# Thirty-three full expert tiles of five batches, not twenty-five of four, inside the last routing round, and a cadence of four tiles for the last stages

## The chip, the core and the metric

The kernel runs on one core of a Trainium2 chip. The metric is the device time of one execution in microseconds (us). TensorE (PE) multiplies, VectorE (DVE) and ScalarE (ACT) read its results out of PSUM, GpSimd (POOL) issues the indirect DMAs, and SyncE (SP) issues the plain ones.

## What is computed

Eight batches of 512 tokens of width 128 go through an attention block and then a mixture-of-experts block. Only the second half of that matters here: each token picks two of eight experts, and its two results are added, weighted by the gate, to a kept row.

```python
probs = softmax(t @ router_w)                      # 8 experts
vals, idx = top_k(probs, 2)
w = vals / sum(vals)                               # gate
hid = silu(t @ w1[e]) * (t @ w3[e])
y = sum over the two experts of w * (hid @ w2[e])
out = x + layernorm(res + y)                       # the last stage of a batch
```

## The kernel before

**Rounds.** A batch passes four stages, a, p, m and f, one round each, and each round runs the stages of up to four batches side by side. Stage f routes a batch: it finishes the attention output, normalises, takes the two best experts of each token (on DVE), ranks the tokens within their expert, and sends 8 blocks of 128 token rows to `token_rows` in HBM (`f_send0` to `f_send7`, on POOL). The last round holds stage f of batch 7 alone.

**Tiles.** All routed rows are worked in 71 tiles of 128 rows of one expert. A tile step k does, on PE, the transpose of tile k's rows (L1109), the eight matmuls of the hidden layer of tile k-1 (`hidden`, L1116) and those of the output of tile k-3 (`down`, L1125). I call the start of the transpose of step k T(k). ACT copies the transposed rows, copies the expert's weights (L1263) and does the silu (L1248). DVE begins its step k with `take_dest` of tile k (L1753, L1754; it waits for the tile's rows and for the send of tile k-8, whose buffers it takes over), then does `gated` of tile k-1 (L1759) and `result` of tile k-3 (L1764, into `k_rows`). POOL sends the result of tile k-3 to `result_rows` with one indirect DMA (L1360). `hidden` of tile n needs `gated` of tile n-2. SP loads the rows of tile k when tile k-8 has been transposed (`load_rows`, L772), so it runs eight steps ahead.

**Early and late tiles.** The rows of the first `SOON` = 4 batches fill at least 4 x 8 - 7 = 25 whole tiles (`EARLY`). Those can start before batch 7 is routed. The other 46 need the counts of all batches: DVE plans them (`plan3` to `plan8`), and SP waits for the plan and for all sends before it loads the first of them. `LAST_ORDER` is a table that writes out for each engine where its tile steps stand between the steps of stage f in the last round. `GROUPS` says at which tile steps PE, ACT and SP read the next tile numbers into registers.

**Last stages of a batch.** When a batch's results are in HBM, SP loads them in two halves (`load_results`, L787, 2 DMAs of 128 KB each, after the wait for the sends of the first `tiles_before_end_of(b)` tiles). DVE adds the two results (`add_pair`, L1771), adds the kept row (`add_kept`, L1775), takes statistics (L1781) and mean and variance (L1788 to L1792), POOL raises to the power -1/2 (`invert`, L1369), ACT centres the four blocks (L1269), and DVE scales and adds (`finish`, L1799). `FINAL_AT[b]` is the step number of batch b, and each part has a lag to it. A step number n there is the tile step k = n + 2. So DVE adds the pair in step FINAL_AT + 2, SP loads in its step FINAL_AT + 5 (POOL's `invert` too), and DVE finishes in step FINAL_AT + 11.

```python
FINAL_AT = [41 + 5 * b for b in range(NB - 1)]
LOAD_AT, SUM_AT, STATS_AT, MEAN_AT, POW_AT, CENTRE_AT, OUT_AT, STORE_AT = 3, 1, 2, 3, 3, 4, 9, 20
def tiles_before_end_of(b):
    return EARLY + NE if b < SOON - 1 else NE * (b + 1) + NE - 1
```

## Time and profile before

| | |
|---|---|
| three runs | 698.15, 699.35 and 699.73 us, median 699.35 |
| the profiled execution | 696.38 us, its span 694.2 us |
| PE, busy share of the span | 88% |
| DVE | 73% |
| ACT | 59% |
| POOL | 49% |
| mean granted TensorE clock | 0.934 |

The profiled execution is 2.97 us below the median of the three runs, and 2.2 us of it lie outside the span. The tiles begin at 544.2 us of the span. The busy shares are averages over stages that have different limits; in the stretch of the tiles the waits and the order of each engine's queue tell more than the shares.

### The profile page before, as it was taken

The numbers are of one execution on the slowest core, as the hardware profiler recorded it, in microseconds if no ns is written. First come the engines' busy times: TensorE is split into PE (matmuls) and PEld (weight loads), VectorE is DVE, ScalarE is ACT, GpSimd is POOL, SyncE is SP. The second block draws the span as 40 slices with busy tenths as digits, with TensorE's granted clock in tenths as the row PEclk, the third lists the DMA queues.
The fourth block names the chain that finished last, engine by engine and source line by source line (L and its number), as shares of the span: only waits on it lengthen the run. The fifth ranks groups of instructions, "written<-read, shape, count | busy, mean of one in ns | idle before, by whom it ended". The sixth has DMA issues, their size and how long they took to land.

```text
span 694.2 us, 15645 instructions
## 1 busy us (share of the span) xinstructions
PE 609.9 (88%) x5186; PEld 364.6 (53%) x5186; DVE 506.8 (73%) x1616; ACT 412.0 (59%) x826; POOL 339.6 (49%) x388
## 2 busy tenths in 40 slices
PE   8887599999999899999999999879998887899980
PEld 3444345455545455454544545434343486899970
DVE  4456877786897898689779878677688356457894
ACT  3223158566658656565765657454564676688971
POOL 0043246058527835752873565165014056767783
PEclk9988879999999999999999999977898999999995
DMA  6200000000100000010000001001232013345653
GB/s 174 78 0 1 0 1 1 2 1 1 35 2 1 14 23 1 1 35 3 1 19 19 1 1 35 2 2 36 77 109 70 14 58 111 99 113 166 176 156 91
DMA packets 35616, 30.05 MB, mean 43 GB/s; under 512 B 6160, under 2 KB 32720, under 8 KB 35520
## 3 DMA queue, kind: packets, MB, share of 16 engines
q1 hardware_dynamic: 31216, 19.65, 10.1%
q0 software_dynamic: 4320, 9.38, 4.0%
q8 instruction: 45, 0.74, 0.4%
q14 instruction: 35, 0.29, 0.1%
HBM read 17.54 MB, written 12.57 MB: 43 GB/s over the span
## 4 chain that ended last, share of the span: by engine, by line
PE 64%; DVE 14%; ACT 9%; issue 7%; POOL 5%; DVEq 0%; POOLq 0%; ACTq 0%
PE wide L1116 9%; PE small L933 7%; PE small L921 5%; PE wide L895 4%; PE wide L1125 4%; ACT pT L1216 4%; PE wide L868 4%; PE wide L886 4%; PE wide L843 3%; PE small L957 3%; PE wide L877 3%; PE small L986 3%; PE small L971 2%; DVE nmax L1421 2%; PE small L1010 2%
## 5 line engine op out<-in xcount | busy, mean ns | idle before, releaser
L1421 DVE TENSOR_REDUCE nmax<-wide 128x2 f32<-128x256 f32 (+3 forms) x256 | 200.1, 817 | 43.7 <-PE wide L886 42.5
L1216 ACT ACTIVATE pT<-wide 128x1024 f32<-128x1024 f32 (+1 forms) x192 | 161.6, 883 | 41.3 <-PE wide L895 40.4
L1360 POOL DMA_INDIRECT result_rows<-k_rows,dest x71 | 69.9, 984 | 49.5 <-DVE k_rows L1764 26.6
L933 PE MATMUL small<-pT,v_pad 128*5 128x512 f32 (+3 forms) x1024 | 85.2, 478 | 2.7 <-ACT pT L1216 2.7
L1351 POOL DMA_INDIRECT token_rows<-m_row,place_u x64 | 62.5, 977 | 45.4 <-issue 16.4
L1302 POOL TENSOR_TENSOR a_rstd<-a_ve,neg_half 128x4 f32<-128x4 f32 x16 | 16.5, 1029 | 117.3 <-DVE a_ve L1407 117.3
L895 PE MATMUL wide<-qT,kT 32*128 32x384 bf16 (+3 forms) x512 | 71.5, 312 | 0.0
L886 PE MATMUL wide<-kT,qT 32*128 32x256 bf16 (+3 forms) x512 | 70.5, 314 | 0.0
L877 PE MATMUL wide<-future_T,idb 128*128 128x128 bf16 (+1 forms) x384 | 62.6, 246 | 7.9 <-DVE nmax L1421 4.6
L868 PE MATMUL wide<-future_sb,idb 128*128 128x128 bf16 (+1 forms) x384 | 64.1, 250 | 5.7 <-ACT pT L1216 2.8
L1145 ACT ACTIVATE oT_g<-small 128x512 f32<-128x512 f32 x32 | 19.1, 597 | 79.7 <-PE small L933 79.7
L933 PEld LDWEIGHTS small<-pT,v_pad 128*5 128x5 f32 x1024 | 25.8, 92 | 59.8 <-issue 50.3
L1759 DVE TENSOR_TENSOR a_work<-a_work,wide 128x256 f32<-128x256 f32 x71 | 29.7, 418 | 32.6 <-PE wide L1125 16.7
L877 PEld LDWEIGHTS wide<-future_T,idb 128*128 128x128 bf16 x384 | 28.6, 99 | 36.4 <-issue 15.8
L1125 PE MATMUL wide<-a_p_sb,a_work 128*128 x284 | 43.2, 275 | 0.6 <-DVE k_rows L1764 0.6
L1116 PE MATMUL wide<-a_work,p_hT_sb 128*128 128x128 f32 x280 | 38.0, 279 | 4.8 <-ACT a_work L1242 3.5
L868 PEld LDWEIGHTS wide<-future_sb,idb 128*128 128x128 bf16 x384 | 29.8, 101 | 22.7 <-issue 11.5
L1116 PE MATMUL wide<-a_work 128*128 128x128 f32 x288 | 38.8, 278 | 2.4 <-issue 2.2
L1125 PEld LDWEIGHTS wide<-a_p_sb,a_work 128*128 128x128 f32 x284 | 37.3, 192 | 0.8 <-issue 0.8
L1116 PEld LDWEIGHTS wide<-a_work,p_hT_sb 128*128 128x128 f32 x280 | 34.0, 192 | 7.0 <-ACT a_work L1242 4.4
L1116 PEld LDWEIGHTS wide<-a_work 128*128 128x128 f32 x288 | 35.3, 193 | 3.4 <-issue 3.0
L895 PEld LDWEIGHTS wide<-qT,kT 32*128 32x128 bf16 x512 | 20.1, 92 | 29.6 <-issue 16.8
(254 smaller groups left out, 1260.6 us busy)
## 6 DMA issues: line engine op xcount, KB each, us to landing
a_qkv_sb<-token_rows SPq DMA_DIRECT2D x71, 72.0 KB, 1.8
x<-L_attn_x SPq DMA_DIRECT2D x8, 256.0 KB, 3.4
w<-L_ffn_w SPq DMA_DIRECT2D x2, 1024.0 KB, 7.3
out<-x SPq DMA_DIRECT2D x16, 128.0 KB
result_rows<-k_rows,dest POOLq DMA_INDIRECT x71, 2.6
token_rows<-m_row,place_u POOLq DMA_INDIRECT x64
a_p_sb<-L_ffn_w SPq DMA_DIRECT2D x8, 128.0 KB, 4.6
yin_own<-result_rows SPq DMA_DIRECT2D x8, 128.0 KB
```

What stands on the lines that cost most here:

```text
L868: pe.matmul(bank[:, i * T + lo:i * T + lo + len(blocks) * P], idb[:, :], future_sb[:, 0:len(blocks), :], start=True, stop=False, skip_grou ...
L877: pe.matmul(diagonal, idb[:, :], future_T[:, :, :] if len(blocks) > 1 else future_T[:, 0, :], start=True, stop=False, skip_group_check=True)
L886: return pe.matmul(bank_of(ring, max_name(g, n))[:, at:at + keys], qT1[rows, m.parity, g, tile * P:(tile + 1) * P], kT[rows, m.parity, g, ...
L895: return pe.matmul(bank_of(ring, exp_name(g, s))[:, at:at + queries_from(tile)], kT[rows, m.parity, g, tile * P:(tile + 1) * P], qT2[rows, ...
L921: last = pe.transpose(bank[0:rows, t * P:(t + 1) * P], source(t), ident)
L933: last = pe.matmul(bank[32 * r:32 * r + HD + 1, k * P:T], v_pad[:, m.parity, k, g * R + r, :], probs, start=(k == 0), stop=(k == NT - 1), ...
L1116: last = pe.matmul(wide[:, tile.half, j * P:(j + 1) * P], w_now[tile.half][:, j * P:(j + 1) * P], x_T[:, tile.half, :], start=True, stop=True)
L1125: last = pe.matmul(y_bank(tile), hid_T[:, tile.half, h * P:(h + 1) * P], w2_sb[:, e, h, :], start=(h == 0), stop=(h == FH - 1))
L1216: act.activation(pT[:, g % 2, part, at:at + n].rearrange("p (n q) -> p n q", n=2), in_, ACT.Exp, scale=SCALE_B).then_inc(ring.free(step), 1)
L1351: pool.indirect_dma_start(token_rows[:, :], bass.IndirectOffsetOnAxis(ap=place_u[:, n, t:t + 1], axis=0), m_row[:, n, t, :], None).then_in ...
L1360: pool.indirect_dma_start(result_rows[:, :], bass.IndirectOffsetOnAxis(ap=dest[:, tile.buf:tile.buf + 1], axis=0), y_rows[:, tile.buf, :], ...
L1421: ins = dve.tensor_reduce(nmax[:, tile, heads], bank[:, :, at:at + keys_up_to(tile)], AX, ALU.max, negate=True)
```

## The change

`SOON` goes from 4 to 5. So `EARLY` goes from 25 to 33 and `LATE` from 46 to 38. The last round holds 33 tile steps instead of 25, and `LAST_ORDER` is written anew. The reads of tile numbers stand at steps 0, 24, 33 and 57 (before: 0, 25 and 49). The padding rows are written at SP's step 29 (before: 21). The last stages of batches 0 to 6 start at step numbers 45, 49, 53, 57, 61, 65, 69 (before: 41, 46, 51, 56, 61, 66, 71). Since `EARLY` grows, the load of batches 0 to 3 waits for the first 41 tiles (before: of batches 0 to 2 for the first 33).

```diff
 LAST_ORDER = {
     "PE": """
-        tile f_pv2 tile f_o1 f_pv3 tile f_o2 f_o3 tile f_oT tile f_up tile tile tile f_tT tile f_logits
...
+tile f_pv2 tile f_o1 f_pv3 tile tile f_o2 f_o3 tile f_oT tile f_up tile tile tile tile f_tT tile tile f_logits tile tile f_rank tile tile tile tile tile tile tile plan tile tile tile tile tile tile tile tile tile tile tile""",
...
-SOON = 4
+SOON = 5
 EARLY = SOON * NE - (NE - 1)
 LATE = TILES - EARLY
...
-PADS_AT = 21
-GROUPS = {0: EARLY, EARLY: 24, EARLY + 24: LATE - 24}
+PADS_AT = 29
+GROUPS = {0: 24, 24: EARLY - 24, EARLY: 24, EARLY + 24: LATE - 24}
...
-FINAL_AT = [41 + 5 * b for b in range(NB - 1)]
+FINAL_AT = [45 + 4 * b for b in range(NB - 1)]
...
-    b = (n - lag - FINAL_AT[0]) // 5
+    b = (n - lag - FINAL_AT[0]) // 4
...
-                experts.update(read_tiles(pe, 1, 0, EARLY, NE - 1))
+                experts.update(read_tiles(pe, 1, 0, GROUPS[0], NE - 1))
```

The POOL queue in the last round, from the tile results behind stage f's `m_row` on (three more stand ahead of that before, five now). `token_rows` are the sends of batch 7, `result_rows` those of tiles, and `a_rstd` and `p_rstd` are what `invert` writes. Before:

```order
L1360 DMA result_rows<-k_rows,dest 10112x128 x4
L1351 DMA token_rows<-m_row,place_u 34688x144 x3
L1360 DMA result_rows<-k_rows,dest 10112x128
L1351 DMA token_rows<-m_row,place_u 34688x144 x2
L1360 DMA result_rows<-k_rows,dest 10112x128
L1351 DMA token_rows<-m_row,place_u 34688x144 x2
L1360 DMA result_rows<-k_rows,dest 10112x128
L1351 DMA token_rows<-m_row,place_u 34688x144
L1360 DMA result_rows<-k_rows,dest 10112x128 x34
L1369 TENSOR_TENSOR a_rstd<-a_ve,neg_half 128x4
L1360 DMA result_rows<-k_rows,dest 10112x128 x5
L1369 TENSOR_TENSOR p_rstd<-p_ve,neg_half 128x4
```

The same place of the POOL queue in the changed kernel:

```order
L1355 DMA result_rows<-k_rows,dest 10112x128 x5
L1346 DMA token_rows<-m_row,place_u 34688x144 x3
L1355 DMA result_rows<-k_rows,dest 10112x128
L1346 DMA token_rows<-m_row,place_u 34688x144 x2
L1355 DMA result_rows<-k_rows,dest 10112x128 x2
L1346 DMA token_rows<-m_row,place_u 34688x144 x2
L1355 DMA result_rows<-k_rows,dest 10112x128
L1346 DMA token_rows<-m_row,place_u 34688x144
L1355 DMA result_rows<-k_rows,dest 10112x128 x34
L1364 TENSOR_TENSOR a_rstd<-a_ve,neg_half 128x4
L1355 DMA result_rows<-k_rows,dest 10112x128 x4
L1364 TENSOR_TENSOR p_rstd<-p_ve,neg_half 128x4
```

Ten tile results stand ahead of the first token send now, not seven; one more tile result stands between the sends; and from the first `invert` on there are four tile results from one to the next, not five.

DVE's queue in the steps of batch 0's `finish`, where the names are those of the batches' result buffers (`yin_own` of batches 0 and 1, `kT` of 2 and 3). Before, with `finish` in a step of its own:

```order
L1759 TENSOR_TENSOR a_work<-a_work,wide 128x256
L1764 TENSOR_SCALAR k_rows<-wide,a_qkv_sb 128x128
L1753 COPY a_qkv_sb<-a_qkv_sb 128x1
L1754 CAST dest<-a_qkv_sb 128x1
L1799 SCALAR_TENSOR_TENSOR x<-yin_own,a_rstd,x 128x128 x4
L1759 TENSOR_TENSOR a_work<-a_work,wide 128x256
```

And in the changed kernel:

```order
L1754 TENSOR_TENSOR a_work<-a_work,wide 128x256
L1759 TENSOR_SCALAR k_rows<-wide,a_qkv_sb 128x128
L1748 COPY a_qkv_sb<-a_qkv_sb 128x1
L1749 CAST dest<-a_qkv_sb 128x1
L1770 TENSOR_TENSOR kT<-kT,res 128x512
L1794 SCALAR_TENSOR_TENSOR x1<-yin_own,a_rstd,x1 128x128 x4
L1754 TENSOR_TENSOR a_work<-a_work,wide 128x256
```

`finish` now falls into the same step as the `add_kept` of the batch two later, and no step is left without a part of a last stage.

## Rows read from the trace of the kernel before

**Rows 1.** Timeline of PE, last round: start, length, line, operation, [idle before <-releaser].

```profile
565.03 0.66 PE L921 MATMUL small<-idf,m_row 128*128 128x128 f32 x4 [1.12 <-POOL m_row L1343]
...
571.95 0.19 PE L1068 MATMUL small<-sel,before_sb 128*128 128x32 bf16 x1 [1.06 <-DVE sel L1604]
...
595.95 1.13 PE L1116 MATMUL wide<-a_work,p_hT_sb 128*128 128x128 f32 x8 [0.94 <-ACT a_work L1242]
...
601.14 0.30 PE L1109 MATMUL wide<-idf,a_qkv_sb 128*128 128x128 f32 x1 [0.71 <-issue]
```

**Rows 2.** Timeline of PE, transposes that begin tile steps 26, 31 and 49.

```profile
602.68 0.27 PE L1109 MATMUL wide<-idf,a_qkv_sb 128*128 128x128 f32 x1
...
609.92 0.27 PE L1109 MATMUL wide<-idf,a_qkv_sb 128*128 128x128 f32 x1
...
637.16 0.30 PE L1109 MATMUL wide<-idf,a_qkv_sb 128*128 128x128 f32 x1 [0.85 <-issue]
```

**Rows 3.** Waits, 585 to 600 us (total, times, longest), and DVE's timeline at step 20.

```profile
DVE a_qkv_sb L1753 <- DMA result_rows<-k_rows,dest: 8.8, 5, 2.7
...
595.29 0.15 DVE L1753 COPY a_qkv_sb<-a_qkv_sb 128x1 f32<-128x1 f32 x1 [1.96 <-DMA result_rows<-k_rows,dest]
```

**Rows 4.** Timeline of POOL: the first token send, and the send of tile 12.

```profile
575.00 0.96 POOL L1351 DMA_INDIRECT token_rows<-m_row,place_u  x1 [3.05 <-DVE place_u L1632]
...
591.43 0.96 POOL L1360 DMA_INDIRECT result_rows<-k_rows,dest  x1 [0.30 <-issue]
```

**Rows 5.** Timelines around batch 0's load (DVE, POOL, SP, DVE), and landings of such DMAs.

```profile
617.78 0.34 DVE L1764 TENSOR_SCALAR k_rows<-wide,a_qkv_sb 128x128 f32<-128x128 f32 x1
...
618.88 0.96 POOL L1360 DMA_INDIRECT result_rows<-k_rows,dest  x1 [0.49 <-issue]
...
621.98 0.81 SPq L787 DMA_DIRECT2D yin_own<-result_rows  x2
...
623.43 0.91 SPq L787 DMA_DIRECT2D yin_own<-result_rows  x2
...
628.30 0.68 DVE L1771 TENSOR_TENSOR yin_own<-yin_own 128x512 f32<-128x512 f32 x1
...
DMA to landing us min/median/max: 2.1/2.3/3.8
```

**Rows 6.** Timeline of DVE, five steps with parts of last stages.

```profile
661.77 0.68 DVE L1771 TENSOR_TENSOR q_rows<-q_rows 128x512 f32<-128x512 f32 x1
662.37 0.41 DVE L1759 TENSOR_TENSOR a_work<-a_work,wide 128x256 f32<-128x256 f32 x1
...
663.09 0.68 DVE L1775 TENSOR_TENSOR q_rows<-q_rows,res 128x512 f32<-128x512 f32 x1
663.68 0.41 DVE L1759 TENSOR_TENSOR a_work<-a_work,wide 128x256 f32<-128x256 f32 x1
...
665.18 0.40 DVE L1759 TENSOR_TENSOR a_work<-a_work,wide 128x256 f32<-128x256 f32 x1
...
666.43 0.41 DVE L1759 TENSOR_TENSOR a_work<-a_work,wide 128x256 f32<-128x256 f32 x1
...
668.19 0.41 DVE L1759 TENSOR_TENSOR a_work<-a_work,wide 128x256 f32<-128x256 f32 x1
```

**Rows 7.** Timeline of POOL from tile 48's send to tile 70's, the last.

```profile
643.65 0.98 POOL L1360 DMA_INDIRECT result_rows<-k_rows,dest  x1 [0.49 <-issue]
...
661.50 1.04 POOL L1369 TENSOR_TENSOR p_rstd<-p_ve,neg_half 128x4 f32<-128x4 f32 x1
...
667.88 0.97 POOL L1360 DMA_INDIRECT result_rows<-k_rows,dest  x1 [0.30 <-DVE x L1799]
668.86 1.63 POOL L1369 TENSOR_TENSOR a_rstd<-a_ve,neg_half 128x4 f32<-128x4 f32 x1
670.68 1.12 POOL L1360 DMA_INDIRECT result_rows<-k_rows,dest  x1 [0.20 <-issue]
...
678.82 0.96 POOL L1360 DMA_INDIRECT result_rows<-k_rows,dest  x1 [0.31 <-issue]
```

More of the change, by code:

```diff
@@ L202 @@
     "PE": """
-        tile f_pv2 tile f_o1 f_pv3 tile f_o2 f_o3 tile f_oT tile f_up tile tile tile f_tT tile f_logits
-        tile tile f_rank tile tile tile tile tile plan tile tile tile tile tile tile tile tile""",
+tile f_pv2 tile f_o1 f_pv3 tile tile f_o2 f_o3 tile f_oT tile f_up tile tile tile tile f_tT tile tile f_logits tile tile f_rank tile tile tile tile tile tile tile plan tile tile tile tile tile tile tile tile tile tile tile""",
     "ACT": """
-        tile f_pv2 tile f_pv3 tile tile f_oT tile tile f_sq tile tile f_tT tile tile tile f_exp
-        tile tile tile tile tile tile tile tile tile tile tile tile tile""",
+tile f_pv2 tile f_pv3 tile tile tile f_oT tile tile tile f_sq tile tile f_tT tile tile tile tile f_exp tile tile tile tile tile tile tile tile tile tile tile tile tile tile tile tile tile tile""",
     "DVE": """
-        tile plan3 tile f_o1 tile f_o2 f_o3 tile tile f_up tile f_ms tile tile tile f_logits f_route0 tile
-        f_route1 f_route2 f_route3 f_at f_rank tile plan4 tile plan5 tile plan6 tile plan7 tile tile plan8 tile tile
-        tile tile tile tile tile tile""",
+tile plan3 tile f_o1 tile tile f_o2 f_o3 tile tile f_up tile tile f_ms tile tile tile tile f_logits f_route0 tile f_route1 f_route2 f_route3 f_at f_rank tile plan4 tile tile plan5 tile plan6 tile plan7 tile tile tile plan8 tile tile tile tile tile tile tile tile tile tile tile""",
     "POOL": """
-        tile tile tile tile tile tile f_rs f_t0 f_t1 tile tile tile tile f_send0 f_send1 f_send2 tile f_send3 f_send4
-        tile f_send5 f_send6 tile f_send7 tile tile tile tile tile tile tile tile tile tile tile tile""",
+tile tile tile tile tile tile tile tile f_rs f_t0 f_t1 tile tile tile tile tile f_send0 f_send1 f_send2 tile f_send3 f_send4 tile tile f_send5 f_send6 tile f_send7 tile tile tile tile tile tile tile tile tile tile tile tile tile tile tile tile""",
 }
```

## The prediction, written before the changed kernel ran

> **What bounds the kernel now.** I read the waits of the tile stretch first, then the timelines of PE, DVE and POOL side by side, then SP's. The reader should see three regimes there. In the middle of the tiles PE is never idle: steps 26 and 31 begin at 602.68 and 609.92 us [rows 2], so a step costs 7.24 / 5 = 1.448 us, and PE sets the pace. In the last round two other things do. Stage f of batch 7 is a chain, and PE waits in it, 1.12 us for the normalised rows and 1.06 us for the selection [rows 1]. Behind it DVE waits 8.8 us in five waits for the landing of tile results [rows 3]: POOL's eight token sends stand in its queue, and `take_dest` of tile k needs the send of tile k-8. In the last 35 us it is POOL again: from 643.65 to 678.82 us its queue hardly rests [rows 7]. Last comes a tail that starts with the send of tile 70 at 678.82 us: load of batch 7, its last stage, the store. It is 694.2 - 678.8 = 15.4 us and nothing of it changes.
>
> So the time is T(47) + (T(47) to the last send) + the tail. By rows 2, T(47) is 602.68 + 21 x 1.448 = 633.1 us before, and from there to the last send it is 45.7 us.
>
> **Eight tiles moved ahead of the late plan: nothing by itself.** A tile costs PE 1.448 us on either side of the plan. It would pay if PE ran out of early tiles before the late rows were there. Before, PE comes to step 25, its first late tile, and waits 0.71 us [rows 1], marked as issue; step 49, in the middle of the late tiles with all rows in SBUF, has the same kind of wait, 0.85 us [rows 2]. Both are steps at which tile numbers are read into registers. I take them as that read, and no gap for rows is left for the eight tiles to fill.
>
> **The reads.** Before, two stand in the steps (25 and 49); now three (24, 33, 57). That adds one, between 0 and 0.85 us. The one at 24 reads nine numbers and falls just ahead of a stall that PE has in any case (next part), so I take 0. If that stall is gone, it costs 0.7.
>
> **Stage f.** The table puts 10, 12 and 14 tiles ahead of `f_tT`, `f_logits` and `f_rank`, before 8, 9 and 11. What `f_tT` waits for starts with the squares on ACT, the mean on DVE and the power on POOL; all three stand two tiles ahead of `f_tT` (at 6 and 8 before, at 8 and 10 now), and POOL must first send the result of the step ahead of them. Between `f_logits` and `f_rank` there are two tiles, as before. So the waits of 1.12 and 1.06 us stay. The added step between `f_tT` and `f_logits` has no wait to cover. I take 0.1 us of gain, from 0 to 2.2 if both waits went.
>
> **Token sends and the release of PE.** POOL's sends follow each other by 1.264 us: the send of tile 12 is number 13 behind the first token send, (591.43 - 575.00) / 13 [rows 4]. It landed at 595.29, 3.9 us after its issue, which was the last wait of the five [rows 3]; PE's `hidden` at 595.95 hangs on it [rows 1]. In the changed queue the three sends that matter behind the rank (tiles 13, 14 and 15 for steps 21, 22, 23) are numbers 10, 12 and 13. Number 13 stays number 13: eight token sends cost POOL the same 10.1 us wherever they stand. What can be won is the slow landing. Tile 32's send was landed and seen by SP within 621.98 - 618.88 = 3.1 us [rows 5]; with that or less it would be 0.8 us earlier or more; SP's padding writes now fall into this stretch, so some landings may be slow again. I take 1.1, from 0.3 to 1.4.
>
> The front then gains 0.1 + 1.1 = 1.2 us: T(47) = 631.9.
>
> **Batch 0 is loaded too late for its addition.** This is the added wait. Before, tile 32 must have landed: its `result` begins at 617.78, its send at 618.88, and SP issues the load at 621.98 [rows 5]. T(35) is 615.7, so the load can go T(t+3) + 6.3 us for the last tile t that it needs. The second half goes out from 623.43 on; its second DMA, issued some 0.45 us later, lands after 2.3 us: 4.25 us from the first issue to all there. DVE wanted it at 628.30, T(43) + 1.0, and it had been there for 2 us. Now the load needs tile 40, and the addition stands in step 47. The load goes at T(43) + 6.3 = T(47) + 0.5 and is all there at T(47) + 4.7. DVE wants it at T(47) + 1.0 and waits 3.7 us. Queued behind it on DVE are `gated` of tile 46 and `result` of tile 44. The addition takes 662.37 - 661.77 = 0.60 us [rows 6], so `gated` begins at T(47) + 5.3 and ends 0.35 later. `hidden` of tile 48 needs it and would have begun at T(49) + 0.1 = T(47) + 3.0: **PE stalls 2.7 us**. Batches 1 to 3 need the same 41 tiles and come 4, 8 and 12 steps later; no wait.
>
> **POOL's last stretch.** Before, POOL does 22 sends and 4 `invert` from 643.65 to 678.82. One `invert` adds (670.68 - 667.88) - 1.3 = 1.5 us [rows 7]. So a send takes (35.17 - 6.0) / 22 = 1.33 us. After the change `invert` stands every four tiles. Five tile sends and one `invert` fit into five PE steps, 8.1 against 7.2 us, less badly than four and one into four, 6.8 against 5.8; both overrun, so once it has started POOL does not come to rest. It starts at the send of tile 47, ahead of the first `invert`. By rows 6 a DVE step without extras is 663.09 - 662.37 = 0.72 us, and the parts of a last stage add 0.60, 0.59, 0.78, 0.53 and 1.04 us. From `gated` at 5.3: 0.6 to the end of step 47, then three steps with 0.59, 0.78 and 0.53, to T(47) + 10.0. The send begins 1.1 us behind the start of `result` [rows 5], at T(47) + 10.8. Then come 23 sends and 5 `invert`: 23 x 1.33 + 5 x 1.5 = 38.1 us. The last send is at T(47) + 48.9, before 45.7: **3.2 us more**, in which the 2.7 us above are contained.
>
> What if DVE is slower than that? Four steps and one batch are now 4 x 0.72 + 3.54 = 6.4 us, against 5.8 of PE. Over the 16 steps 55 to 70 that is 25.7 us for 23.2, and the last `result` comes out near T(47) + 46 to 47. It needs POOL 1.1 us later, so DVE ends a little ahead of POOL's 48.9. The two are close, and what delays either shows in full; I keep 1 us for it at the upper end.
>
> **The sum.** -1.2 + 3.2 = +2.0 us. The profiled execution would go from 696.4 to 698.4 us. Since it lay 2.97 us below the median of its runs, I put the difference on the median: 699.35 + 2.0 = 701.3 us.
>
> **Two rules weighed.** Both results lie inside the forecast's own range (below), and I give each 0.1 of its chance. POOL's `invert` is 1.04 us long once and 1.63 us once, with the same shape [rows 7]. The Trainium skill (GPSIMD Engine Reference, section 1, Specifications) says that GpSimd shares its SBUF interfaces with VectorE and is disturbed by VectorE instructions with two SBUF inputs. The two additions of a last stage and `finish` are such, and they come closer together now, so the rule speaks against the change. By it all five would take 1.63 us, 0.2 above what I used for each, and the time would be 702.3; the row of 1.04 us also lay beside such an addition, at 661.77 [rows 6], so the trace bears it out only half.
> The Trainium skill (DMA: Bandwidth & Descriptors, section Anatomy of one DMA) gives a fixed cost of about 2.0 us for a GpSimd DMA plus its bytes by 436 GB/s, an estimate of 2.15 us for 64 KB. The landing of 3.9 us in the trace does not agree. With 2.15 us for tile 40 instead of the 3.1 us from 618.88 to 621.98, the wait for batch 0 would be some 0.9 us shorter, and the time 700.4.
>
> **Rivals.**
> *The back is covered.* The load of batch 0 goes earlier than I work out or PE's two steps of lead take the wait up, and POOL gets its rests. Then only the front is left, -1.2 to 0 us: 698.2 to 699.4 us. For it speaks that the busy shares are below one; against it, that the addition stands only 4 steps behind the send it needs (before: 8). Chance 0.25.
> *The landings get slow.* Loads of results, stores and tile rows come closer. A landing of 3.9 us for tile 56 or 60 puts `take_dest` of step 64 or 68 behind by 1 to 2 us, and PE with it; this decides the time if DVE and not POOL ends last. 703.3 us. Chance 0.15.
> *Faster, the waits of the last round go.* If the one more tile result between the sends lets `take_dest` pass and both waits of stage f are covered, the front gains 1.2 + 2.2 and the back costs little: about 696.5 us. It needs POOL to have rest in the round, and rows 4 show none between 575 and 591 us. Chance 0.12.
> *Forecast,* 701.3 us, of itself 700.0 to 702.6: chance 0.48.
> That the change does not do what it says can be left out: the step numbers are constants.
>
> **Chances and range.** About 0.2% of the time, 1.4 us, is what a measurement tells from no change. Faster by more: the 0.12 and 0.03 of the covered case, 0.15. Within: 0.22 of the covered case and 0.08 of the forecast's lower edge, 0.30. Slower: 0.55. The range is 698.0 to 703.6 us; it leaves out the faster case and the ends.
>
> **What would show it.** Right: DVE idle for some 3.7 us ahead of the first `add_pair`, behind a DMA from `result_rows`; the step with it 2.7 us longer on PE; T(47) near 632; POOL without rest from there to its last send near 680.7; five waits on `take_dest` in the last round again. Wrong: T(47) more than 2 us earlier (the last round gained), or no wait ahead of the first `add_pair`, or a wait of PE at step 33 for late rows.

## The result, and the profile after it

The changed kernel takes 703.94 us (median of 20 runs, 696.09 to 708.32), the kernel before 699.19 us (median of 20). The ratio is 1.0077, with a 95% interval of 1.0053 to 1.0101: it is slower, by under 1%. A second set of the same two kernels gave 1.0052 (1.0024 to 1.0081). The ratios compare fast executions alone, without the few slow ones (here one of 1083.18 us of the kernel before and one of 708.32 us of the changed one), so they are not the quotients of the medians beside them. The direction was forecast and the size was not: 701.3 us was the likeliest value, 703.6 us the upper end of the range. The profiled execution of the changed kernel took 703.88 us, with a span of 701.6 us.

Times vary from execution to execution of one kernel, and so do profiles. The tiles began at 544.2 us in the profile of before, at 547.9 us in the one of after. A later section shows that the kernel before alone varies by as much. So I reckon all marks from the first tile's transposes. By T(n) I mean the transposes that begin step n, and "last send" is POOL's send of tile 70. The rank product is the matmul of `sel` and `before_sb` in stage f, at 571.95 us in [rows 1].

The names of after stand five lines higher in the code than those of before (`turn_rows` is L1104, `hidden` L1111, `down` L1120, `result` L1759, `add_pair` L1766).

| from the first tile's transposes, us | rank product | T(28) to T(34) | T(47) | T(47) to last send | to the end of the span |
|---|---|---|---|---|---|
| before | 27.77 | 8.69 | 88.93 | 45.71 | 150.02 |
| before, second profile | 27.77 | 8.69 | 88.01 | 45.75 | 149.00 |
| after | 32.98 | 9.54 | 89.37 | 49.08 | 153.72 |
| the changed kernel, second profile | 32.98 | 9.93 | 89.11 | 49.66 | 153.82 |

Against the first profile of before the loss is 3.7 and 3.8 us, nearly all of it behind tile 47. Against the second it is 4.7 and 4.8 us, with 1.4 and 1.1 us of it ahead of tile 47. So one profile each leaves the front uncertain by about 1 us. The back is much firmer, 45.71 and 45.75 us before. There stands what [rows 5] answered to before, batch 0's load. These are VectorE's rows of after (start, length, line, operation, and in brackets the idle time before it and its releaser), then SP's issue of that load, then TensorE's rows:

```profile
637.86 0.34 DVE L1759 TENSOR_SCALAR k_rows<-wide,a_qkv_sb 128x128 f32<-128x128 f32 x1
...
642.07 0.69 DVE L1766 TENSOR_TENSOR yin_own<-yin_own 128x512 f32<-128x512 f32 x1 [3.75 <-DMA yin_own<-result_rows]
642.68 0.41 DVE L1754 TENSOR_TENSOR a_work<-a_work,wide 128x256 f32<-128x256 f32 x1
```

```profile
636.85 1.64 SPq L782 DMA_DIRECT2D yin_own<-result_rows  x2
```

```profile
640.15 0.27 PE L1104 MATMUL wide<-idf,a_qkv_sb 128*128 128x128 f32 x1
643.20 1.13 PE L1111 MATMUL wide<-a_work 128*128 128x128 f32 x8 [2.78 <-issue]
...
644.70 0.42 PE L1104 MATMUL wide<-idf,a_qkv_sb 128*128 128x128 f32 x1
644.91 1.91 PE L1111 MATMUL wide<-a_work,p_hT_sb 128*128 128x128 f32 x8
...
647.47 0.42 PE L1104 MATMUL wide<-idf,a_qkv_sb 128*128 128x128 f32 x1
...
649.14 0.27 PE L1104 MATMUL wide<-idf,a_qkv_sb 128*128 128x128 f32 x1
```

VectorE waited 3.75 us for the rows (forecast: 3.7), TensorE stood for 2.78 us (forecast: 2.7). What the forecast did not have stands behind it. The transposes take 0.42 us instead of 0.27, eight products 1.91 us instead of 1.06, and the step from 644.70 us takes 2.77 us instead of 1.45. The windows of after (window, its length, busy time and instructions of the engines, granted clock, DMA share, GB/s) say why, and which engine then sets the end:

```profile
643.20:649.00 5.80, 5.80 (x37) 5.80 (x38) 4.81 (x27) 2.72 (x7) 2.86 (x3) 0.71 0.58 169
649.00:686.00 37.00, 32.70 (x270) 30.58 (x269) 35.94 (x174) 29.58 (x83) 28.67 (x28) 0.99 0.59 172
```

The granted clock is 0.71 of full speed in the 5.8 us behind the stall, a mixture of the two levels, 1.2 and 2.4 GHz, and 0.99 afterwards. And from 649 us to the last send VectorE is busy for 35.94 of 37 us, GpSimd for 28.67. In all of that stretch VectorE has the first two of these marked rests and no other. The third row is already the tail:

```profile
649.41 0.42 DVE L1754 TENSOR_TENSOR a_work<-a_work,wide 128x256 f32<-128x256 f32 x1 [0.22 <-ACT a_work L1243]
...
660.95 0.42 DVE L1754 TENSOR_TENSOR a_work<-a_work,wide 128x256 f32<-128x256 f32 x1 [0.16 <-PE wide L1120]
...
688.38 1.14 DVE L1794 SCALAR_TENSOR_TENSOR x<-q_rows,p_rstd,x 128x128 f32<-128x128 f32 x4 [2.38 <-POOL p_rstd L1364]
```

GpSimd, which the forecast took for the engine that sets the end [rows 7], rests now and then: its send behind tile 48's waits 1.36 us, and tile 69's waits for VectorE's result.

```profile
651.92 1.03 POOL L1355 DMA_INDIRECT result_rows<-k_rows,dest  x1 [0.20 <-issue]
654.31 0.96 POOL L1355 DMA_INDIRECT result_rows<-k_rows,dest  x1 [1.36 <-issue]
...
685.06 0.96 POOL L1355 DMA_INDIRECT result_rows<-k_rows,dest  x1 [0.71 <-DVE k_rows L1759]
686.33 0.96 POOL L1355 DMA_INDIRECT result_rows<-k_rows,dest  x1 [0.30 <-issue]
```

In the last round the two waits of stage f are what they were, 1.12 and 1.05 us [rows 1]. The waits for the landing of tile results have the total that [rows 3] showed for before, 8.8 us in five. For 580 to 618 us of after:

```profile
DVE a_qkv_sb L1748 <- DMA result_rows<-k_rows,dest: 8.9, 7, 3.1
```

The step that reads tile numbers has moved. Step 33 has now the gap that step 25 had before, and step 24, where nine numbers are read, has none. The rows of steps 24, 32 and 33:

```profile
602.17 0.42 PE L1104 MATMUL wide<-idf,a_qkv_sb 128*128 128x128 f32 x1
...
614.53 0.27 PE L1104 MATMUL wide<-idf,a_qkv_sb 128*128 128x128 f32 x1
616.74 0.30 PE L1104 MATMUL wide<-idf,a_qkv_sb 128*128 128x128 f32 x1 [0.59 <-issue]
```

The first of these rows is a slow one, 0.42 us. The clock fell in the front too. VectorE had waited 3.12 us for a landing and TensorE stood for 2.17 us behind it. The window behind that stall was granted 0.63:

```profile
599.79 1.74 PE L1111 MATMUL wide<-a_work 128*128 128x128 f32 x8 [2.17 <-issue]
```

```profile
599.79:604.38 4.59, 4.59 (x25) 4.36 (x26) 2.01 (x11) 1.51 (x4) 3.37 (x5) 0.63 0.56 166
```

In the second profile of the changed kernel it is the same behind a stall of 2.62 us (0.72 from 594 to 600 us). In both profiles of before the granted clock was 1.00 there.

### The profile page after: what moved, and what is told of

It reads as the page before. It is cut to its first block, busy times and chain, and to the rows that moved or that the text cites. A ratio compares the mean times of both kernels' runs of the same rounds, so it can differ in the third digit from the quotient of the medians.

```text
span 701.6 us, 15648 instructions
## 1 busy us (share of the span) xinstructions
PE 613.3 (87%) x5186; PEld 366.8 (52%) x5186; DVE 508.3 (72%) x1616; ACT 411.2 (59%) x826; POOL 337.9 (48%) x388
## 4 chain that ended last, share of the span: by engine, by line
PE 63%; DVE 12%; issue 9%; POOL 8%; ACT 7%; DVEq 0%; POOLq 0%; ACTq 0%
PE small L928 8%; PE wide L1111 7%; PE small L916 5%; PE wide L890 5%; PE wide L863 4%; PE wide L881 4%; PE wide L872 3%; PE small L952 3%; PE wide L838 3%; PE wide L1120 3%; ACT pT L1211 3%; PE small L981 3%; PE small L966 3%; DVE nmax L1416 2%; PE small L1019 2%
## 5 line engine op out<-in xcount | busy, mean ns | idle before, releaser
L1111 PE MATMUL wide<-a_work 128*128 128x128 f32 x288 | 39.8, 282 | 7.4 <-issue 5.9
L1120 PE MATMUL wide<-a_p_sb,a_work 128*128 x284 | 44.5, 280 | 0.6 <-DVE k_rows L1759 0.5
L1111 PEld LDWEIGHTS wide<-a_work 128*128 128x128 f32 x288 | 36.0, 196 | 8.9 <-issue 7.6
L1111 PE MATMUL wide<-a_work,p_hT_sb 128*128 128x128 f32 x280 | 39.3, 285 | 0.9 <-ACT p_hT_sb L1258 0.5
L1120 PEld LDWEIGHTS wide<-a_p_sb,a_work 128*128 128x128 f32 x284 | 38.3, 196 | 1.0 <-issue 1.0
L1111 PEld LDWEIGHTS wide<-a_work,p_hT_sb 128*128 128x128 f32 x280 | 35.5, 199 | 2.7 <-issue 2.0
```

The source lines that it names most:

```text
L1111: last = pe.matmul(wide[:, tile.half, j * P:(j + 1) * P], w_now[tile.half][:, j * P:(j + 1) * P], x_T[:, tile.half, :], start=True, stop=True)
L1120: last = pe.matmul(y_bank(tile), hid_T[:, tile.half, h * P:(h + 1) * P], w2_sb[:, e, h, :], start=(h == 0), stop=(h == FH - 1))
```

## Experiments: one part of the change at a time

My theory after the result: the late load of batch 0 is the price, and it is paid in full because VectorE has no rest behind it. (The experiments bear out its first half and not the second.) The rivals: the tighter cadence, the new placing of the 33 tiles, or something ahead of the tiles. Four runs went together, beside 34 runs of before (median 699.12 us).

**The changed kernel once more.**

> The changed kernel once more, unaltered, to have a second profile of it. In the two profiles so far the last round begins at 544.2 us (before) and 547.9 us (changed), and from there to the end it is 150.0 and 153.7 us. Theory A (the whole loss arises from the last round on; the 3.7 us ahead of it are the spread of single executions): from the start of the last round to the end 153.7 us again, within 1 us; the start itself anywhere from 543 to 549. Rival B (the larger plan for five batches also delays the rounds ahead): the start at 547.9 again, within 0.7 us. Both: 3.5 to 5 us over the kernel before.

Measured: 701.99 us, ratio 1.0052 (1.0024 to 1.0081). Its marks are in the table above: the first tile at 545.98 us, and from there to the end 153.8 us as in the first profile. Theory A holds, and B falls. The 2.9 us over before are less than the 3.5 to 5 expected. VectorE's wait is 4.14 us, TensorE's 3.17 us.

**The last stages begin at tile 48.** Batch 0's rows should then be in before they are wanted.

```diff
-FINAL_AT = [45 + 4 * b for b in range(NB - 1)]
+FINAL_AT = [48, 51, 55, 58, 62, 65, 69]
-    b = (n - lag - FINAL_AT[0]) // 4
-    return b if 0 <= b < NB - 1 and FINAL_AT[b] + lag == n else None
+    return FINAL_AT.index(n - lag) if n - lag in FINAL_AT else None
```

> The changed kernel with the last stages of batches 0 to 4 one to three steps later (48, 51, 55, 58, 62, 65, 69), so that the results of the first 41 tiles are loaded before batch 0's addition. Theory A (the wait for batch 0 starts the loss: 3.8 us on DVE, 2.8 us on PE, and then steps at half of TensorE's clock): no wait ahead of the first add_pair over 0.5 us, no step with a transpose of 0.42 us behind it, and the last send comes 2 to 3 us earlier, counted from the start of step 47: 46 to 47 us instead of 49.1. Total 2 to 3 us below the changed kernel. Rival B (POOL's last stretch is full in any case, and a later start only packs it closer): last send 48.5 to 49.5 us behind step 47 as now, total within 1 us of the changed kernel.

Measured: 701.44 us, 1.0038 (1.0016 to 1.0060). The wait shrinks to 0.64 us and the stall is gone, yet from T(47) to the last send it still takes 47.99 us, against 49.1 and 49.7 with the wait and 45.7 before. Avoiding the wait by starting later gives back only a part, between what the theory (46 to 47 us) and its rival (48.5 or more) expected. I put the rest down to VectorE's work for seven last stages, which is then pressed into fewer steps; no run separates that.

**The kernel before, with a last stage every four tiles.**

```diff
-FINAL_AT = [41 + 5 * b for b in range(NB - 1)]
+FINAL_AT = [45 + 4 * b for b in range(NB - 1)]
-    b = (n - lag - FINAL_AT[0]) // 5
+    b = (n - lag - FINAL_AT[0]) // 4
```

> The kernel before with the changed step numbers for the last stages alone (45, then every four tiles); 25 early tiles and their order stay. Batch 0's load needs 33 tiles and does not come too late. Theory A (the cadence by itself costs little, since POOL's run starts 2.7 us earlier than in the changed kernel): last send 46 to 47 us behind step 47, total +0.3 to +1.5 us over the kernel before. Rival B (the cadence is the loss, DVE and POOL cannot follow four steps per batch): last send 48 us or more behind step 47, total +2.5 us or more.

Measured: 698.97 us, 1.0010 (0.9986 to 1.0035). The cadence alone costs nothing that can be measured. T(47) to the last send is 46.40 us, 0.7 more than before.

**The changed kernel with the placing of before.** The first 25 tiles stand in the last round where they stood, the other eight behind them. This is TensorE's list, the other three engines' lists likewise:

```diff
-tile f_pv2 tile f_o1 f_pv3 tile tile f_o2 f_o3 tile f_oT tile f_up tile tile tile tile f_tT tile tile f_logits tile tile f_rank tile tile tile tile tile tile tile plan tile tile tile tile tile tile tile tile tile tile tile
+tile f_pv2 tile f_o1 f_pv3 tile f_o2 f_o3 tile f_oT tile f_up tile tile tile f_tT tile f_logits
+tile tile f_rank tile tile tile tile tile plan tile tile tile tile tile tile tile tile tile tile tile tile tile tile tile tile
```

> The changed kernel, but with stage f of batch 7 at the same tile positions as in the kernel before, and the eight further tiles at the end of the last round. Theory A (the new positions of stage f cost 1.0 us, in the step ahead of f_o2 and in the two tiles ahead of f_tT): rank at 27.8 us behind the round's start, step 34 some 1 us earlier than in the changed kernel, total 0.5 to 1.5 us below it. Rival B (the front depends on POOL's eight token sends alone): step 34 and the total within 0.5 us of the changed kernel. Rival C (stage f later is better, since more tiles cover it): total 1 us or more above it.

Measured: 702.90 us, 1.0050 (1.0021 to 1.0078). The rank product is back at 27.77 us. VectorE's wait of 3.75 us and TensorE's of 2.78 us are there all the same, and the whole is 1.5 us shorter in the profile (152.24 us to the end). Only 0.6 us of that lie ahead of tile 47 (T(47) is 88.79 us). The other 1.0 us lie behind it, and there the placing is the same as in the changed kernel. What differs is the clock: behind a stall of the same length it did not fall, and the next step took 1.45 us and not 2.77.

```profile
643.00 1.13 PE L1116 MATMUL wide<-a_work 128*128 128x128 f32 x8 [2.78 <-issue]
...
644.41 0.27 PE L1109 MATMUL wide<-idf,a_qkv_sb 128*128 128x128 f32 x1
...
645.86 0.27 PE L1109 MATMUL wide<-idf,a_qkv_sb 128*128 128x128 f32 x1
```

```profile
642.80:648.80 6.00, 5.64 (x48) 5.47 (x49) 5.97 (x33) 4.15 (x11) 3.69 (x4) 1.00 0.61 171
```

So a stall of 2.78 us can lower the clock and need not; the runs do not show what decides it.

## Experiments: the late load alone, and the clock behind it

Four more, beside 35 runs of before (median 698.89 us).

**The kernel before with only its load late.** The number of tiles that must have landed before the loads of batches 0 to 2 goes from 33 to 37. That is the relation which 41 landings have to a last stage four steps later.

```diff
-    return EARLY + NE if b < SOON - 1 else NE * (b + 1) + NE - 1
+    return EARLY + NE + 4 if b < SOON - 1 else NE * (b + 1) + NE - 1
```

> The kernel before, with one edit: the results of the batches 0 to 2 may be loaded only when the senders of the first 37 tiles are known to have landed, not of the first 33. It is the relation that the changed kernel has (41 landings for a load placed four steps later), without its 33 tiles in the round and without its cadence. Theory (the late load is the price): VectorE waits 3.5 to 4 us for batch 0's rows at its step 44 or so, TensorE stalls 2.5 to 3 us once; from the mark of tile 47's transposes (or 43's, where the wait now stands before it) to the last result send 2 to 3.5 us more than the 45.7 of before, the time 0.3 to 0.5% over before. Rival 1 (the wait is absorbed, since VectorE and GpSimd catch up until the last send): same stall, last send within 0.7 us of before, time within 0.1%. Rival 2 (most of the loss is from the 33 tiles in the round or from packing by fours): the same as rival 1 in the time.

Measured: 704.06 us, 1.0052 (1.0023 to 1.0082). One changed number, without any of the added tiles or the cadence, gives a loss as large as that of the whole change. VectorE's row, and TensorE's with the same slow step behind the stall:

```profile
634.49 0.69 DVE L1771 TENSOR_TENSOR yin_own<-yin_own 128x512 f32<-128x512 f32 x1 [3.35 <-DMA yin_own<-result_rows]
```

```profile
635.61 1.13 PE L1116 MATMUL wide<-a_work 128*128 128x128 f32 x8 [2.38 <-issue]
637.33 0.42 PE L1109 MATMUL wide<-idf,a_qkv_sb 128*128 128x128 f32 x1
640.10 0.27 PE L1109 MATMUL wide<-idf,a_qkv_sb 128*128 128x128 f32 x1
```

The stall lies ahead of T(47) here. So T(43) is the mark to reckon from: to the last send it is 55.93 us, against 51.51 before. These 4.4 us are more than the 2 to 3.5 that I had expected.

Where do they arise? From T(43) to T(47) it takes 10.05 us instead of 5.80, so 4.25 of the 4.42 us are there by tile 47. From T(47) to the last send it takes 45.89 us, against 45.71 before. TensorE, which did a step every 1.45 us ahead of the stall, hands its delay on. VectorE, on the other hand, does rest behind it, as it does before (1.89 us there):

```profile
666.98 0.15 DVE L1753 COPY a_qkv_sb<-a_qkv_sb 128x1 f32<-128x1 f32 x1 [2.00 <-DMA result_rows<-k_rows,dest]
```

So it is not for want of a rest on VectorE that the delay is paid here.

**The same with 39 landings.** Two runs of it came to chips that were then slower; they are in the next section. This is the third:

> The kernel before with the results of the batches 0 to 2 loaded only when the senders of the first 39 tiles are known to have landed. Only a chip that runs the kernel before in 699 us tells the size. Theory (a late load is paid in full at the end, one to one): VectorE waits some 6.3 us, two tile steps of 1.45 us longer than the 3.35 us with 37; from tile 43's transposes to the last result send 58 to 60 us (51.5 before, 55.9 with 37), the time 0.8 to 1.1% over before. Rival (the end takes a part back): 57 us or less, and 0.6% or less. On a chip that takes about 798 us for the kernel before: 1.002 to 1.005, as the two runs there.

Measured: 707.37 us, 1.0128 (1.0094 to 1.0163), and 59.12 us from T(43) to the last send. Both are in or above the range of the theory. VectorE waits 5.81 us, TensorE 4.84 us:

```profile
638.59 0.69 DVE L1771 TENSOR_TENSOR yin_own<-yin_own 128x512 f32<-128x512 f32 x1 [5.81 <-DMA yin_own<-result_rows]
```

```profile
639.71 2.05 PE L1116 MATMUL wide<-a_work 128*128 128x128 f32 x8 [4.84 <-issue]
642.41 0.42 PE L1109 MATMUL wide<-idf,a_qkv_sb 128*128 128x128 f32 x1
```

The three kernels make a scale: waits of 0, 3.35 and 5.81 us delay the last send by 0, 4.4 and 7.6 us, about 1.3 us for each us of wait. The rival, that the end takes a part back, falls: 7.3 of the 7.6 us are there by T(47), and from T(47) to the last send it takes 46.01 us. The 7.3 us are TensorE's stall of 4.84 us and 2.5 us of slow work behind it; the 4.25 us above are 2.38 and 1.9 us. So what is paid is TensorE's stall, about 1 us less than VectorE's wait, plus the lower clock.

**TensorE kept busy in the stall.** In the kernel with 37 landings it repeats the transposes of tile 45, with the same values in the same place.

```diff
                 pe.wait_ge(xT_free, tile.n + E_CREDIT)
+                for _ in range(20 if tile.n == 45 else 0):
+                    pe.transpose(wide[:, 0, T:T + P], x_rows[:, tile.buf, 0:D], idf[:, :])
```

> The kernel with the late load alone (37 landings), in which TensorE repeats the transposes of tile 45 twenty times, 0.11 us each in a row, while it would have stood idle. On a chip that runs the kernel before in 699 us, theory (about 1.3 us of the loss is the lower clock after the stall): no transposes of 0.42 us behind it, the step from tile 46's to 47's 1.5 us and not 2.77; from tile 43's transposes to the last result send 54.2 to 55.0 us and not 55.9; the time 0.1 to 0.2% under the 1.0052 of the late load alone. Rival (VectorE or GpSimd sets the pace there): 55.6 to 56.2 us and 1.005. On a chip that takes about 798 us for the kernel before: 0.997 to 1.001, as the two runs there.

Measured: 701.70 us, 1.0053 (1.0019 to 1.0087), beside 697.65 us of before. TensorE's rows, and the clock of the window around them:

```profile
629.76 2.35 PE L1110 MATMUL wide<-idf,a_qkv_sb 128*128 128x128 f32 x20
631.95 0.27 PE L1111 MATMUL wide<-idf,a_qkv_sb 128*128 128x128 f32 x1
632.59 1.13 PE L1118 MATMUL wide<-a_work 128*128 128x128 f32 x8 [0.37 <-issue]
...
634.00 0.27 PE L1111 MATMUL wide<-idf,a_qkv_sb 128*128 128x128 f32 x1
...
635.45 0.27 PE L1111 MATMUL wide<-idf,a_qkv_sb 128*128 128x128 f32 x1
```

```profile
629.80:638.00 8.20, 7.67 (x68) 7.25 (x66) 5.95 (x30) 4.74 (x14) 3.30 (x4) 1.00 0.58 168
```

VectorE still waits 3.53 us for its rows. But the clock stays at 1.00, the step behind takes 1.45 us, and T(43) to the last send is 53.93 us, 2.0 us less than without the repeats. T(47) comes 1.5 us of that earlier; the other 0.5 us arise later, where VectorE waits 1.22 us for a landing instead of 2.00. In the profile some 1.5 to 2 us of the 4.4 are thus the clock behind the stall. And with the clock up a wait of 3.53 us delays the last send by 2.4 us, not by 3.5. The times don't confirm it: the ratio is the same as without the repeats, and its interval of ±0.34% is wider than the 0.15 to 0.3% in question. So this share rests on one profile. That the repeats kept the clock up is likely and not shown, since with the placing of before it stayed up behind a stall without them.

**The same in the changed kernel,** nine repeats at tile 49.

> The changed kernel with one edit: TensorE repeats the transposes of tile 49 nine times more, 0.27 us each, so that it works through the 2.8 us in which it stood for VectorE's wait for batch 0's rows, and writes the same values in the same place. Theory (the stall also costs the clock afterwards): the granted clock stays at its upper level, the transposes of tiles 50 and 51 take 0.27 us and not 0.42, steps 50 to 52 take 1.5 us each and not 2.8 and 1.7; the mark of tile 52 comes 1 to 1.6 us earlier from the first tile's; the last result send 0 to 1 us earlier, since GpSimd's sends bind that stretch; time 0 to 0.15% under the changed kernel. Rival (the slow steps are VectorE's and GpSimd's backlog and not the clock): marks of tiles 51 and 52 unchanged within 0.3 us, although the transposes are short.

Measured: 702.57 us, 1.0046 (1.0020 to 1.0072). The nine repeats took only 1.15 us in a row and not 2.4. TensorE still stood 2.09 us, and the clock stayed up. Since it did so with the placing of before too, without any repeats, that is not proof of their effect:

```profile
633.88 1.15 PE L1105 MATMUL wide<-idf,a_qkv_sb 128*128 128x128 f32 x9
...
637.23 1.13 PE L1113 MATMUL wide<-a_work 128*128 128x128 f32 x8 [2.09 <-issue]
...
638.64 0.27 PE L1106 MATMUL wide<-idf,a_qkv_sb 128*128 128x128 f32 x1
```

T(52) comes 1.9 us earlier, the last send 0.8 us (T(47) to it: 48.82 us against 49.08 and 49.66). Here the clock matters less. In the 5.8 us behind the stall VectorE is busy for 5.76 us, with the clock up; it has its last stages to do in those very steps, and little more could be gained.

**Both edits of the first series together:** the placing of before, and the last stages from tile 48.

> The changed kernel with both earlier edits together: the placing of the 25 tiles in the last round as in before, with the eight more behind them, and the last stages of the batches at tiles 48, 51, 55, 58, 62, 65, 69, so that batch 0's rows are in when they are wanted. If the two prices are apart (front 1 to 1.5 us in the stall and the clock behind it, back 1 us), from the first tile's mark to the end it takes 151.3 us (152.24 with the old places, less 0.9) and the time is 0.2 to 0.3% over before. If the old placing removes a cost that the late start then gives back in the packed end, it is like the late start alone, 152.8 and 0.4%. Faster than before would need 149.7 or less, which neither theory gives.

Measured: 699.76 us, 1.0012 (0.9985 to 1.0039): of all kernels with five batches' tiles the nearest to before, and not faster than it. The forecast of 0.2 to 0.3% was a little high. With it the four combinations can be set side by side:

| ratio to before | batch 0 waits (from tile 45) | it doesn't (from tile 48) |
|---|---|---|
| placing of the change | 1.0077 and 1.0052 | 1.0038 |
| placing of before | 1.0050 | 1.0012 |

With the mean of the two at the upper left, 1.0065, the placing costs 0.15 and 0.26% down the columns, the wait 0.27 and 0.38% along the rows. Each single step is about as large as the intervals; that both pairs say the same is what speaks for it. In the left column the profiles differ by the clock behind the stall as well (1.0 us of 1.5), so there the price of the placing is not a clean one.

**The kernel before once more.** Does the later start of the tiles belong to the change?

> The kernel before, unchanged: a second profile and a second set of times. If the 3.7 us by which the changed kernel was later than before at the first tile's transposes (547.9 against 544.2, and 546.0 to 548.3 in the three other kernels with five batches) belong to the change, this profile has the mark at 543.5 to 544.5 again. If they are only where TensorE's granted clock happened to fall in the first 150 us, the mark lies anywhere from 543.5 to 548.5, and the time within 0.1% of before.

Measured: 698.25 us, 0.9994 (0.9969 to 1.0019), and the first tile's transposes at 548.80 us. These are GpSimd's rows of the third round's power step in the two profiles of the same kernel, first before, then its second profile:

```profile
149.97 1.01 POOL L1302 TENSOR_TENSOR p_rs<-p_ms,neg_half 128x4 f32<-128x4 f32 x1 [4.99 <-DVE p_ms L1544]
```

```profile
154.30 1.01 POOL L1302 TENSOR_TENSOR p_rs<-p_ms,neg_half 128x4 f32<-128x4 f32 x1 [4.98 <-DVE p_ms L1544]
```

Of the 4.6 us by which the first tiles differ, 4.3 arise by 150 us of the span and stay. The kernels with four batches have the mark of the first tile at 543.9 to 548.8 us, those with five at 542.1 to 548.3 us. Nothing ahead of the tiles is part of the change.

## Experiments on slower chips

Eight runs came to two chips that took 799.57 and 797.50 us for the kernel before, beside the 697 to 699 us of all other runs. One of the two was the chip on which the 39 landings were measured later, at 697.65 us for before. So it is not a property of a chip that stays. I have no profile of before from there. In the eight that I have the first tile's transposes come at 605.4 to 612.9 us and not at 542 to 549, so some 60 of the 100 us arise ahead of the tiles. In the profile of the 39 landings from there the DVE, ACT and POOL busy sums are within 1% of those elsewhere, but all engines have long gaps for which no releaser on the core is seen. ScalarE has two of them in a row in the last round, and VectorE its own:

```profile
646.87 0.38 ACT L1248 ACTIVATE a_work<-wide 128x256 f32<-128x256 f32 x1 [6.44 <-remote]
654.31 0.37 ACT L1242 ACTIVATE a_work<-wide,g_sb 128x128 f32<-128x128 f32 x1 [7.06 <-remote]
```

```profile
653.58 0.42 DVE L1759 TENSOR_TENSOR a_work<-a_work,wide 128x256 f32<-128x256 f32 x1 [10.77 <-remote]
```

> The changed kernel with the old placing of the first 25 tiles in the last round and the last stages of the batches at tiles 48, 52, 55, 59, 62, 66, 70: as the variant with 48 to 69, but with the later batches one tile further apart, as near to a stage every four tiles as the buffers allow. If the packing (every 3.5 tiles) costs something, it is faster than that variant's 1.0012: 0.999 to 1.001, and 150.5 us from the first tile's mark to the end. If not, 1.001 to 1.002 and 151.8 us. A version faster than before by over 0.2% is expected by neither.

> The same with the changed kernel's own placing of the 33 tiles. Where the placing costs what the earlier pairs say (1.0052 to 1.0077 against 1.0050 with the wait, 1.0038 against 1.0012 without it, so 0.1 to 0.3%), this is 0.1 to 0.3% slower than the variant beside it. Where it costs nothing and those pairs were chance, both agree within 0.1%.

> The changed kernel, unchanged, beside the three others and the kernel before. On a chip that runs the kernel before in 699 us: 1.005 to 1.008 as twice so far. On one that takes 799.6 us for it, this tells whether the 33 tiles in the round are worth something there: 0.990 to 0.995 if the two variants' gain there (0.9908 and 0.9916) came of those tiles, 1.000 to 1.005 if it needs the later last stages too.

| kernel | first slow chip (before 799.57) | second (before 797.50) |
|---|---|---|
| 39 landings | 1.0005 (0.9976 to 1.0034) | 1.0045 (1.0013 to 1.0078) |
| 37 landings, kept busy | 0.9968 (0.9934 to 1.0002) | 1.0003 (0.9972 to 1.0035) |
| placing of before, stages at 48, 52, 55, 59, 62, 66, 70 | 0.9916 (0.9877 to 0.9954) | 0.9981 (0.9951 to 1.0011) |
| placing of the change, the same stages | 0.9908 (0.9873 to 0.9944) | not run |
| the changed kernel | not run | 0.9978 (0.9943 to 1.0012) |

On the first of them the question of packing had no answer; the placing, 0.9908 against 0.9916, made no difference. There the changed kernel and its variants are level with before or up to 0.9% ahead, and the late load costs 0.0 to 0.5% instead of 1.3%. That fits gaps of 7 to 11 us beside which a wait of some us is hidden, but I did not show that, and the two chips differ among themselves by 0.65% for one kernel. Neither the cause of the gaps nor the gain is settled.

## Why the prediction was right in direction and too small

**The added wait: right.** 3.75 and 4.14 us measured for 3.7, TensorE's stall 2.78 and 3.17 for 2.7; no wait for batches 1 to 3.

**The front: the step that failed.** T(47) was to be 1.2 us earlier. It came 0.4 and 0.2 us later than in the first profile of before, and 1.4 and 1.1 us later than in the second. Over all profiles beside a before of 697 to 699 us, T(34) is 70.0 us on the average of six kernels with 25 tiles and 70.1 us on that of six with 33. The gain was nothing.
- *The slow landing, -1.1 us: this is the term that was wrong.* The row of 3.9 us looked like a chance that could go. In after such a landing does take about 2.7 us (send at 599.05, seen at 601.79), and nothing is won: VectorE's total wait for them is 8.9 us, before 8.8. It is 8.3 to 9.4 us in eight other profiles with 25 or 33 tiles, and 11.3 and 11.0 us in the changed kernel's second and in the one with nine repeats. The eight token sends stand in GpSimd's queue in all of them, which would explain a constant total; no run changes their number. Behind these waits the clock fell too, in both profiles of the changed kernel.
- *The added register read, priced at 0: right in the sum.* Three reads stand in the steps now, but the one at step 24 shows no gap. The one at step 33 costs what the one at step 25 did before (0.59 and 0.71 us). T(28) to T(34) is 9.48 to 9.93 us in all six profiles with 33 tiles and 8.69 or 8.70 us in all six with 25 because the read of 25 lies ahead of T(28) and that of 33 behind it; T(28) comes 0.85 us earlier on the average, and by T(34) nothing of it is left. The forecast had the read at 24 hidden by a stall. With the placing of before no stall stands there, and it shows no gap either. It reads nine numbers, the others 22 or 24.

**The back, T(47) to the last send: 48.9 forecast, 49.08 and 49.66 measured.** The number held, its reason did not, so that it fits is in part luck. The sum was made for GpSimd, with 1.33 us a send. GpSimd needed 1.27 us, (669.11 - 666.58) / 2 for sends in a row, and rested, while VectorE did not. The forecast had VectorE's last result at T(47) + 46 to 47 and kept 1 us for it; it came at 685.00 us, T(47) + 47.8.

**The lower clock behind the stall: missing from the sum.** It has no term in the prediction. With the late load alone it was worth some 1.5 to 2 us in the profile. In the changed kernel it was 0.3 to 0.8 us at the last send by the kernel with the repeats, and 1.0 to 1.6 us by the one with the placing of before.

**The rivals.** That the back is covered (698.2 to 699.4) fell with the wait. The faster case fell with the waits of stage f, both still there. *The landings get slow* gave a time near the measured one, 703.3, but for another reason: no tile's landing held VectorE between 649 us and the last send of after. Of the two rules that were weighed, neither gave the size: the `invert` instructions took 1.04 to 1.52 us in the last stretch, none 1.63, and the wait was the longer one, 3.75 us, not 2.8.

**The sum by what the runs showed:** against the first profile of before, front +0.2 to +0.4, back +3.4 to +3.9, to the end 3.7 and 3.8 us; against the second, front +1.1 to +1.4 and the same back, 4.7 and 4.8 us. The medians say 4.75 and 2.87 us, and with the ratios' intervals of ±0.25 to 0.3% all this agrees. By the second set alone the time would have been inside the forecast's range; it is the missing gain of the front that both sets and all profiles show. What remains open is the split of the back's loss between the wait, the clock, the cadence and the placing. They are not additive: the late load alone costs 4.4 us in its profile, the cadence alone 0.7, and the changed kernel, which has both, 3.4 to 3.9. The kernels of this cadence that have the wait need 48.11 to 49.66 us from T(47) to the last send, the one without it, which has 25 tiles in the round, 46.40 us. By that the wait and the clock behind it cost 1.7 to 3.3 us together, where VectorE waits 3.75 to 4.14.

## What to carry to other kernels

Before moving work to an earlier place, look at the first consumer of a transfer that the move leaves late, and follow its wait to the engine that sets the pace there. What counts is the part that reaches that engine (here TensorE's 2.38 of VectorE's 3.35 us), since it has no rest in which to make it up, plus what a lower clock behind the stall adds. Take the engine that sets the end from the window between the wait and the last instruction (35.9 of 37 us busy), not from a sum over the queue that looked fullest before. Waits behind a burst of sends had nearly the same total wherever the burst stood; don't count a part as won because one landing was slow. And before pricing a second occurrence of something, check which one the mark you reckon from has already passed: the read at step 33 is the one of step 25, moved.

## What the runs showed of the hardware

- After TensorE had stood for 2.78 us in an otherwise full stretch of the changed kernel, the granted clock was 0.71 in the 5.8 us that followed. It was 0.71 after 3.17 us in the second profile, 0.71 after 2.38 us and 0.60 after 4.84 us in the kernels with a late load. With the placing of before it stayed at 1.00 after the same 2.78 us. Kept at work through it, or for 1.15 us of it with 2.09 us idle left, it stayed at 1.00 too. Transposes took 0.42 us at the lower level against 0.27, eight products up to 2.05 us against 1.06. I had priced such a stall at its own length.
- A read of tile numbers on TensorE's queue left a gap of 0.46 to 0.98 us with 22 or 24 numbers (steps 25, 33 and 49), of 0.2 to 0.4 us with 14 (step 57), and none that shows with nine (step 24).
- The same transposes of one tile, repeated in a row, took 0.11 to 0.13 us each (twenty in 2.35 us), while one alone is shown with 0.27 us.
- Two profiles of one kernel lay 4.6 us apart at the first tile (544.18 and 548.80 us), 4.3 us of it from the first 150 us. A difference of one profile each ahead of the changed code says nothing.
- One and the same chip took 799.57 us for the kernel before at one time and 697.65 us at another.
